# Attention in a fused convolution chain on one core: the first maxima tile of a step ahead of the scores

## The reference

```python
def _L3_conv_ref(x, q_w, k_w, v_w):
    b, din, h, w = x.shape
    hw = h * w
    xf = x.reshape(b, din, hw)
    Q = jnp.einsum('kc,bcp->bkp', q_w, xf)      # 16 rows
    K = jnp.einsum('kc,bcp->bkp', k_w, xf)      # 16 rows
    V = jnp.einsum('vc,bcp->bvp', v_w, xf)      # 64 rows
    S = jnp.einsum('bkp,bkq->bpq', Q, K)
    A = jax.nn.softmax(S, axis=-1)
    z = jnp.einsum('bpq,bvq->bvp', A, V)
    return z.reshape(b, V.shape[1], h, w)
...
x = x + _L3_conv_ref(_gn(x), L3_conv_q_w, L3_conv_k_w, L3_conv_v_w)
```

## Time and profile before

| | |
|---|---|
| median of three runs | 1657.02 us |
| profiled execution: its own time | 1657.63 us |
| profiled execution: span from first to last instruction | 1655.8 us |
| PE busy | 1591.5 us (96% of the span) |
| DVE busy | 1214.3 us (73%) |
| ACT busy | 1181.3 us (71%) |
| POOL busy | 1112.7 us (67%) |
| reductions of tiles (L759) | 1323 of 617 ns |
| exponentials (L1025) | 700, 901 ns in the mean |
| sums of tiles (L990) | 588 of 608 ns, and 202 ns each to read the sum |

### The profile page before, as it was taken

The page is one execution under the profiler, slowest core; times in us unless marked ns, Lnnn a source line. Parts: engine busy times, 40 slices in busy tenths (PEclk is TensorE's granted clock), DMA queues, the critical chain, the costliest instruction groups (busy, mean ns, idle before and its releaser), DMA issues.

```text
span 1655.8 us, 29770 instructions
## 1 busy us (share of the span) xinstructions
PE 1591.5 (96%) x10979; PEld 824.5 (50%) x10979; DVE 1214.3 (73%) x2338; ACT 1181.3 (71%) x2280; POOL 1112.7 (67%) x910
## 2 busy tenths in 40 slices
PE   4999999999998999999999999999999999999996
PEld 3457457466464344444444444444444444444442
DVE  5866866857847777777777777777777777777750
ACT  2054053053045689999999999999999999999984
POOL 1720720720812378888888888888888888888887
PEclk9999999999999799999999999999999999999999
DMA  2010211201135105000000600000410000000000
GB/s 85 1 40 40 69 40 47 72 29 54 55 43 145 58 7 111 12 13 13 12 13 14 114 12 13 13 12 13 70 58 13 13 12 13 12 8 7 7 7 12
DMA packets 15586, 57.21 MB, mean 35 GB/s; under 512 B 4560, under 2 KB 11088, under 8 KB 13008
## 3 DMA queue, kind: packets, MB, share of 16 engines
q1 hardware_dynamic: 15440, 55.31, 12.5%
HBM read 30.94 MB, written 24.22 MB: 33 GB/s over the span
## 4 chain that ended last, share of the span: by engine, by line
PE 83%; DVE 9%; POOL 3%; issue 2%; ACT 2%; DMA 0%; POOLq 0%; DVEq 0%; ACTq 0%
PE PS L1434 29%; PE PS L1368 15%; PE PS L1407 14%; PE PS L1301 7%; PE PS L1256 5%; PE PS L1246 3%; POOL accP L1162 2%; DVE nmt L759 2%; DVE st L507 2%; PE PS L1356 1%; DVE nmt L766 1%; PE PS L1344 1%; PE PS L1291 1%; PE PS L1290 1%; PE PS L1212 1%
## 5 line engine op out<-in xcount | busy, mean ns | idle before, releaser
L759 DVE TENSOR_REDUCE nmt<-PS 128x1 f32<-128x448 f32 x1323 | 767.0, 617 | 222.4 <-PE PS L1368 221.8
L1162 POOL TENSOR_TENSOR accP<-accP,Pb 128x512 f32<-128x512 f32 x504 | 639.6, 1269 | 87.8 <-ACT Pb L1025 36.9
L1025 ACT ACTIVATE Pb<-PS 128x896 f32<-128x896 f32 (+1 forms) x700 | 626.8, 901 | 83.0 <-PE PS L1407 76.0
L990 ACT ACTIVATE PS<-PS,nmt 128x448 f32<-128x448 f32 x588 | 357.7, 608 | 25.8 <-DVE nmt L759 10.4
L1434 PE MATMUL PS<-Pb,VT 128*64 128x448 f32 x1400 | 323.6, 541 | 1.7 <-ACT Pb L1025 1.2
L1434 PE MATMUL PS<-Pb,xnf 128*64 128x448 f32 x1400 | 322.6, 539 | 0.0
L1368 PE MATMUL PS<-xnp,xin 96*64 96x448 bf16 x1408 | 250.5, 369 | 9.8 <-ACT PS L990 5.3
L1407 PE MATMUL PS<-xin,xnp 99*64 99x448 bf16 x1372 | 244.8, 353 | 0.7 <-ACT Pb L1025 0.6
L1368 PE MATMUL PS<-Ka,Qa 96*64 96x448 bf16 x1372 | 243.3, 353 | 0.9
L1407 PE MATMUL PS<-Qa,Ka 99*64 99x448 bf16 x1372 | 240.4, 353 | 0.0
L1368 PEld LDWEIGHTS PS<-xnp,xin 96*64 96x64 bf16 x1408 | 81.5, 113 | 147.0 <-issue 68.9
(11 more groups left out here) (169 smaller groups left out, 1877.7 us busy)
## 6 DMA issues: line engine op xcount, KB each, us to landing
saved_v<-VT SPq DMA_DIRECT2D x4, 1600.0 KB, 11.3
xin<-in_x SPq DMA_DIRECT2D x4, 1568.0 KB, 6.6
saved_x<-xw SPq DMA_DIRECT2D x4, 1568.0 KB, 5.1
out<-xw SPq DMA_DIRECT2D x28, 224.0 KB, 1.9
saved_parts<-parts SPq DMA_DIRECT2D x4, 1176.0 KB, 8.0
xw<-saved_x SPq DMA_DIRECT2D x21, 224.0 KB, 2.6
xnf<-saved_v SPq DMA_DIRECT2D x2, 1600.0 KB, 17.3
VT<-saved_v SPq DMA_DIRECT2D x2, 1600.0 KB, 16.2
```

The source lines that it names most:

```text
L759: nc.vector.reduce_max(nmt[:, target % 2, b, t:t + 1], PS[0:BLK, bank, 0:CH], X, negate=True).then_inc(mx_free, 1)
L990: return nc.scalar.activation(PS[0:BLK, bank, 0:CH], PS[0:BLK, bank, 0:CH], ACT.Exp, bias=nmt[:, target % 2, b, t:t + 1], accum_out=sm[:, ...
L1025: nc.scalar.activation(Pb[:, j % PSLOTS, 0:m, :], PS[:, 2 * (k % 2):2 * (k % 2) + m, 0:CH], ACT.Exp).then_inc(exp_done, 1)
L1162: nc.gpsimd.tensor_tensor((accQ if j < TO_ACCP else accP)[:, :, REST:CH], (accQ if j <= TO_ACCP else accP)[:, :, REST:CH], Pb[:, j % PSLOT ...
```

## The change

```diff
@@ superblock() of the TensorE program @@
                         pe.wait_ge(exp_done, k + 1)
                         if j:
                             values(j)
-                        for h in range(2):
-                            if k + 2 < NQ * SBS:
-                                if j == NQ - 2 and h == 0:
-                                    pe.wait_ge(mrow_loaded, 16 * ROW_LOADS * (sidx + 1))
+                            if tiles:
+                                max_tile(*tiles.pop(0))
+                        if k + 2 < NQ * SBS:
+                            if j == NQ - 2:
+                                pe.wait_ge(mrow_loaded, 16 * ROW_LOADS * (sidx + 1))
+                            for h in range(2):
                                 scores(k + 2, h)
-                            if tiles and j:
-                                max_tile(*tiles.pop(0))
                         if not j:
                             values(j)
                         for tile in tiles:
                             max_tile(*tile)
```

## The result

The changed kernel takes 1646.04 us in the median of six runs (1645.02 to 1647.29), the kernel before 1657.03 (1655.85 to 1657.96): a ratio of 0.9934, 95% interval 0.9923 to 0.9944. That is 11.0 us less. The profiled execution took 1647.29 us, 10.3 less than that of before.

A forecast was written before the change was run, and what follows sets the result against it. PE was taken to bound the kernel, so only its holes could shrink: 4.9 us at step 5, 2.4 at step 1 and 0.7 in superblock 0, together 8.0 off 1657.02, giving 1649.0 us; range 1647.3 to 1652.7.

The forecast's parts named there:

- What bounds the kernel: Attention part: PE is busy 99.80 of 100 us at full clock, so only its holes can be gained.
- The hole at step 5: Ahead of step 5's second tile, superblocks 1 to 26: 0.24 us falls to about 0.05, 4.9 us gained.
- The hole at step 1: Ahead of step 1's values, superblocks 1 to 26: the 0.09 us hole closes, 2.4 us gained.
- The cost of the exchange itself: Reordered matmuls on PE, 641 steps: taken as nothing; rounding alone bounds it at -6 to +6 us, unrounded starts at +0.6.
- A new wait: First tile asking for its bank 0.19 us sooner: cost 0 in superblocks 1 to 26, at most 0.55 us in superblock 0.
- Superblock 0: Superblock with three tiles in most steps: 0.7 us gained, bounds 0.2 to 1.1.
- The end: Last superblock, where POOL binds: gains still count because POOL idles 0.42 us for ACT behind the last step 5.
- The sum: Whole kernel: -4.9 - 2.4 - 0.7 = -8.0 us, which gives 1649.0 us on the median.
- The range: Whole kernel: 1647.3 to 1652.7 us, from all holes closed wholly to past the case of step 5 alone.
- The weight load behind the values: Rule against the change: a load waiting for its bank directly behind the values loses overlap; slower rival, 1662 to 1670, chance 0.05.

The follow-up runs named there:

- step 4 alone: The kernel before, with the new order (first tile directly behind the values) at step 4 only: 1650.67 us, ratio 0.9967.
- the later transposition: The kernel before, PE's order unchanged, with DVE's transposition back of the denominators at step 4 moved behind the second tile's reduction: 1650.11 us, ratio 0.9957.
- the kernel with all tiles first: The changed kernel, with all tiles of a step ahead of both scores in steps 1 to 24: 1680.37 us, ratio 1.014.

## Why the prediction was wrong, point by point

- **What bounds the kernel**: right that it is PE, wrong that only its holes count. Smaller holes account for some 9.1 of the 10.6 us that the attention gained; the rest is cheaper pairs of matmuls, in steps without a hole.
- **The hole at step 5**: right in mechanism and size. 0.19 of 0.24 us was forecast; step 5 fell from 1.777 to 1.589 us, of which 0.003 is the cheaper pair: 26 x 0.185 = 4.8 us for the 4.9 forecast. Shown from both ends, by step 4 alone and by the later transposition.
- **The hole at step 1**: right in mechanism, with the tile of step 22 as its cause, and too small in size. The values started 0.09 late, and I took that for the price. Steps 0 and 1 became shorter by 0.093 and 0.047 us, of which 0.003 is the cheaper pair. Values whose weight load is held up have their second half 0.43 us behind the first instead of 0.38: it shows in the row of before, 0.60 long where others are 0.55. 26 x 0.137 = 3.6 us instead of 2.4. This is the other mis-sized term of the sum.
- **The cost of the exchange itself**: this is the step that failed. I put the term at nothing, after comparing values to scores with values to a tile, and so bounded a gain away. I had compared the wrong neighbours. What the change makes adjacent is scores and scores, and such a pair was there to be read at step 0 of the kernel before, whose values start at 1030.17:

```profile
1029.80 0.55 PE L1407 MATMUL PS<-Qa,Ka 99*64 99x448 bf16 x4
```

  The two pairs of scores take 0.37 us, by unrounded starts 192 and 188 ns, where every pair of an ordinary step takes 192. With the change 21 steps that had no hole became 1.8 to 3.5 ns shorter each, and steps 1 and 5 have the cheaper pair too. Step 22 went the other way, from 1.325 to 1.329 us: its order of before, with the two half pairs of scores around the tile, already held one pair of 188 ns, and the new order has none. In all it is 26 x 0.059 = 1.5 us less, where the forecast left 0.6 us more at most. It lies within the rounding bound of 6 us that I wrote down and then dropped.
- **A new wait**: right. Tile 1 waits for no bank in superblocks 1 to 26; at step 4 the tile at 1032.57 runs on time. In superblock 0 step 1 lost 0.2 us, and a later tile of that step gave it back, as forecast.
- **Superblock 0**: 45.16 to 44.41 us, some -0.8 for -0.7.
- **The end**: right, the gain passes through to the end: from the last values to the last instruction it is 14.2 us in both kernels.
- **The sum**, from the terms as measured: 4.8 + 3.6 + 1.5 + 0.8 = 10.7 us. The trace has 10.6 from the first values of the attention to the last; the last superblock, which has no tiles, took 0.05 longer. Of the 2.7 us that the forecast of 8.0 lacked, the exchange makes 1.5 and the hole at step 1 makes 1.2.
- **The range** left no room for what two sets of executions differ by. Its low end of 1647.3 was the best case of a sum with both mis-sized terms in it (9.7 us less), and each side of a comparison carries about 1 us from elsewhere (below).
- **The weight load behind the values.** Standing behind the values is no loss: in the changed kernel the weight load for the tile at 1032.57 starts at 1032.19, 0.38 us ahead of it and beside the values, and the tile's row is 0.36 long. What costs is the wait for the bank itself, as the kernel with all tiles first shows: the held tile starts at 1054.69, and the scores behind it only at 1054.90. A held tile, as at step 5, also takes 213 ns to the next start where others take 192.

## What to carry to other kernels

When an engine is full, look for the few steps in which it is not, and follow each back through the in-order engines to the instruction that somebody else had been waiting for; here one tile at step 4 and one at step 22 carried 8.4 of 10.6 us, and the other 22 exchanges only their 3 ns, apart from superblock 0. Before calling an exchange free, compare every pair of neighbours that it makes with every pair that it breaks, to the nanosecond where it is repeated hundreds of times. And when a wait is moved forward in an in-order queue, add up the slack of each place: 0.5 us of slack made it free for one tile, and 0.06 to 0.37 us made it cost 0.08 to 0.38 for the second.

## What the runs showed of the hardware

- A pair of bf16 matmuls with 448 columns costs TensorE 188 ns behind a pair with the same number of rows and 192 behind one with another number (96 and 99 here), at full granted clock. Equal rows removed the difference although the tensors still changed roles. How it is where the two matmuls of a pair differ in their rows, as at step 22 of the kernel before, was not tried apart.
- Float32 values whose first weight load is late lose 0.05 us a second time, inside their own four matmuls (0.43 instead of 0.38 between their halves): in the kernel before, with step 22 in the old order and with the transposition later alike.
- The part ahead of the attention, identical in all kernels, ends at different times. The first values in the changed kernel and in the same kernel again:

```profile
558.55 0.92 PE L1434 MATMUL PS<-Pb,xnf 128*64 128x448 f32 x4
```

```profile
556.11 0.55 PE L1434 MATMUL PS<-Pb,xnf 128*64 128x448 f32 x2
```

In the same two traces, the matmuls at 42 us:

```profile
42.15 5.06 PE L1246 MATMUL PS<-Ka,selb 96*128 96x448 bf16 x13
```

```profile
42.24 3.14 PE L1246 MATMUL PS<-Ka,selb 96*128 96x448 bf16 x12
```

And the busy time from 552 to 555.5 us (the number behind POOL's is the granted clock):

```profile
552.00:555.50 3.50, 3.50 (x23) 1.63 (x20) 0.56 (x5) 0.00 (x0) 0.00 (x0) 0.50 0.00 0
```

```profile
552.00:555.50 3.50, 2.95 (x29) 1.22 (x25) 0.00 (x0) 1.68 (x2) 0.00 (x0) 0.96 0.00 0
```

The starts of the first values lie 2.4 us apart, and the clock accounts for most of it. By unrounded starts the matmuls at 42 us follow one another every 373 ns, and then every 189: the pace of the lower level (1.2 GHz) and of the upper (2.4). It doubles at 47.0 us in the one execution and at 43.7 in the other. The same matmul starts 0.3 us apart ahead of this and 1.8 us apart behind it. The other 0.6 us arises where a stretch at the lower level ends, at 555.7 us in the one and 552.3 in the other. In the first 43 us PE was busy 19.2 and 19.4 us, so its work doesn't tell the two apart; why the level rises earlier in one stays open. The difference is as large as the whole spread of the changed kernel's six runs (2.3 us), so a comparison of a few microseconds is better made between two instructions inside the attention than between totals.
